# A graph layer's gathers in another order on GpSimd's queue, and its node statistics one block nearer

## The reference

```
h = maximum(layernorm(x), 0)                      # 100000 x 160
s, v = h[:, :64], h[:, 64:] as (N, 32, 3)
skip = s @ W_skip0, v @ W_skip1
s, v = s @ W_nl0, v @ W_nl1
w = relu(edge_feature @ W_fc1) @ W_fc2            # 25000 x 224, in five parts
xs, xv = s[dst], v[dst]                           # gathered by edge
tp = products of w, xs, xv and the edge's unit vector
agg = segment_sum(tp, src, N) / 32
out = agg @ W_out + skip
gate: silu on 64 scalars, sigmoid of 32 times the vectors
x + result
```

## Time and profile before

| | us |
|---|---|
| median of 3 runs | 1115.03 |
| lowest and highest run | 1113.84, 1117.93 |
| the profiled execution, device time | 1114.05 |
| its span, first to last instruction | 1112.2 |
| PE, DVE, ACT, POOL busy in the span | 1055.0, 960.1, 911.9, 762.7 |
| first and last scatter start | 147.35, 540.77 |
| first and last residual start | 555.65, 1103.40 |

### The profile page before, as it was taken

The page is one execution under the profiler, slowest core; times in us unless marked ns, Lnnn a source line. Parts: engine busy times, 40 slices in busy tenths (PEclk is TensorE's granted clock), DMA queues, the critical chain, the costliest instruction groups (busy, mean ns, idle before and its releaser), DMA issues.

```text
span 1112.2 us, 29797 instructions
## 1 busy us (share of the span) xinstructions
PE 1055.0 (95%) x8847; PEld 930.5 (84%) x8847; DVE 960.1 (86%) x3525; ACT 911.9 (82%) x2168; POOL 762.7 (69%) x1021
## 2 busy tenths in 40 slices
PE   6899899999999999789799999999999999999996
PEld 5678688888888887678698889999999899989885
DVE  9999789888888896668389899999999999999984
ACT  0796578777787876546699999999999999999994
POOL 6777777777777777775726667676767665667650
PEclk9999899999999999869699999999999999999998
DMA  9999745544455664343488788888888888888863
GB/s 336 403 403 402 255 136 137 143 135 137 139 138 143 216 230 141 109 118 103 139 295 301 281 298 308 306 310 299 312 298 313 296 297 311 302 305 308 301 215 128
DMA packets 108461, 271.14 MB, mean 244 GB/s; under 512 B 13573, under 2 KB 51751, under 8 KB 108364
## 3 DMA queue, kind: packets, MB, share of 16 engines
q1 hardware_dynamic: 87852, 233.20, 59.6%
q0 software_dynamic: 19200, 36.48, 10.8%
q10 hardware_dynamic: 1312, 0.29, 0.1%
HBM read 126.91 MB, written 143.01 MB: 243 GB/s over the span
## 4 chain that ended last, share of the span: by engine, by line
PE 36%; DVE 24%; DMA 21%; issue 7%; POOL 6%; SPq 4%; ACT 0%; DVEq 0%; POOLq 0%; ACTq 0%
DMA xb<-x 20%; DVE n_stat L995 7%; PE bank L1457 6%; DVE ob L1093 6%; DVE ob L1086 5%; PE bank L1486 4%; POOL slots L546 4%; PE bank L1388 3%; PE bank L1474 3%; PE bank L1470 3%; PE bank L1472 3%; PE bank L1494 2%; PE bank L1440 2%; DVE bin_hot L660 2%; PE bank L1527 2%
## 5 line engine op out<-in xcount | busy, mean ns | idle before, releaser
L1302 ACT ACTIVATE nn<-xb,n_bias,n_rstd 128x160 f32<-128x160 f32 x784 | 345.4, 526 | 0.0
L546 POOL DMA_INDIRECT slots<-msg,sidx x200 | 208.1, 1041 | 68.3 <-issue 57.3
L995 DVE BATCH_NORM_STATS2 n_stat<-xb 128x6 f32<-128x160 f32 x784 | 195.9, 313 | 35.6 <-DMA xb<-x 34.7
L1545 PE MATMUL bank<-mg,hot 64*128 64x192 f32 x1568 | 172.3, 338 | 2.4 <-DVE hot L1071 2.4
L530 POOL DMA_INDIRECT xg<-x,dst_i x136 | 136.3, 1002 | 43.9 <-issue 40.7
L1527 PE MATMUL bank<-fwd,nt 128*128 128x160 f32 x784 | 153.6, 319 | 8.9 <-DVE ob L1086 6.4
L595 POOL TENSOR_TENSOR n_rstd<-n_sum,neg_half 128x8 f32<-128x8 f32 x94 | 156.4, 1664 | 7.6 <-POOL n_sum L588 6.9
L1093 DVE TENSOR_TENSOR ob<-ob,xb 128x1280 f32<-128x1280 f32 x98 | 146.2, 1492 | 3.4
L1527 PEld LDWEIGHTS bank<-fwd,nt 128*128 128x128 f32 x784 | 112.5, 190 | 40.0 <-issue 33.1
L1086 DVE SCALAR_TENSOR_TENSOR ob<-sg,bank 128x128 f32<-128x128 f32 x588 | 130.9, 278 | 17.0 <-ACT ob L1320 17.0
L1312 ACT ACTIVATE nt<-bank 128x640 f32<-128x640 f32 x196 | 136.6, 698 | 9.0 <-PE bank L1536 7.3
(11 more groups left out here) (197 smaller groups left out, 2686.5 us busy)
## 6 DMA issues: line engine op xcount, KB each, us to landing
xb<-x SPq DMA_DIRECT2D x97, 640.0 KB, 5.2
out_dram<-ob SPq DMA_DIRECT2D x97, 640.0 KB, 3.3
slots<-blank SPq DMA_DIRECT2D x14, 2744.0 KB
mg<-slots SPq DMA_DIRECT2D x98, 392.0 KB, 4.0
messages<-msg SPq DMA_DIRECT2D x50, 382.8 KB
ef<-edge_feat_t SPq DMA_DIRECT2D x50, 125.0 KB
slots<-msg,sidx POOLq DMA_INDIRECT x200, 3.6
xg<-x,dst_i POOLq DMA_INDIRECT x136, 6.4
```

The costliest lines, as they stand in the source:

```text
L546: pool.indirect_dma_start(slots[:, :], bass.IndirectOffsetOnAxis(ap=sidx[:, m:m + 1], axis=0), msg[:, c, t, 0:MW], None).then_inc(e_sc[c], 16)
L995: done = dve.bn_stats(n_stat[:, u // U, u % U * G + g, :], xb[:, u, g, :])
L1302: last = act.activation(nn[:, u % 2, h, spread_of(g % 4)], xb[:, u, g, order_of(g % 4)], ACT.Relu, bias=n_bias[:, u // U, c:c + 1], scale= ...
L1545: last = pe.matmul(q_z[h][:, t, 0:Z], hot[slots, u % 2, pair, :], mg[slots, u % U, pair, 0:Z], start=False, stop=(h == 0), skip_group_chec ...
```

## The change

Three lines change, in two stages. `FIRST_GATHERS` goes from 112 to 128. Behind the scatters of each group come two gathers until all 200 are made; before, the bound `GE * (p + 11)` made it four behind groups 36 to 39. In the node stage DVE takes the statistics of block i + 5 in round i instead of i + 6, so the loop's first such round is 3 (block 8), and the last 92 (block 97).

```diff
-    FIRST_GATHERS = 112
+    FIRST_GATHERS = 128
...
-                    due = min(NT, max(FIRST_GATHERS + 2 * (p + 1), GE * (p + 11)))
+                    due = min(NT, FIRST_GATHERS + 2 * (p + 1))
...
-                        s, v = i + 6, (u + 6) % XU
-                        measure = macro_exists(s) and macro_exists(i - 2)
+                        s, v = i + 5, (u + 5) % XU
+                        measure = macro_exists(s) and macro_exists(i - 3)
```

## The result

The changed kernel takes **1087.68 us** (median of 4 runs, 1086.12 to 1088.71) where the kernel before took 1116.48 beside it (4 runs, 1113.84 to 1118.47): a ratio of 0.974, with an interval of 0.971 to 0.977. The prediction was 1092.5 in a range of 1087 to 1101. The sign and both mechanisms held, and the time lies near the range's low end: both halves gave more than they were costed at. The profiled execution of after took 1086.12 us, 27.9 less than that of before.

The account below looks back on a forecast made before the run. Bounds: node-row loads in the node stage, POOL's queue with late gathers in the edge stage. 1114.05 - 7.3 + 1.0 - 15.8 = 1091.95 us, taken as 1092.5 with the median's offset; range 1087 to 1101.

Parts of the forecast that it names:

- A: Edge stage: POOL's queue loses its waits for messages, so the node stage starts earlier: -7.3 us, bounded by 0 and -9.
- The slack of the ring: Edge stage: ACT's copy for group 44 finds its message buffer, one of eight, free with 1.5 us to spare.
- B: Node stage's start: PE's first adds stay at the lower clock for longer: +1.0 us, between 0 and +1.7.
- C: Node stage: DVE's waits for node-row loads go, rounds take 5.49 us: -15.8 us.
- the floor of 530.0: Node stage: first to last residual with rounds at PE's 5.47 us, a gain of 17.7 us.
- the slack of the even blocks' bias: Node stage: POOL has an even block's bias ready 2.9 us before ACT reads it, so ACT does not wait.
- R1: Node stage: something other than the load holds rounds, half the excess stays, rounds 5.56 us, total 1098.7 us; chance 0.09.
- R2: Edge stage: the gather change gives nothing, last scatter ends near 541 us, total 1099.3 us; chance 0.06.
- R3: Node stage: waits on node-row loads stay because loads come slower in shorter rounds, total 1107.8 us; chance 0.05.
- R4: Node stage: POOL becomes the bound and ACT waits for the bias, priced at 1145.7 us; chance 0.06.
- The three more steps held for 1.3 us each: Node stage: POOL steps held by DVE, making a pair of blocks take 12.1 us and a round 6.05; priced under R4.
- The price of a ring that runs full: Edge stage: if message buffers run out, ACT and DVE stop a few us while POOL has seven groups; cost nothing.

Follow-up runs that it names:

- e_small_store: The kernel before, statistics still six blocks ahead, storing only 1/8 of each block's output: 1095.61 us (one run).
- e_stats_only: The kernel before with only the statistics moved to block i + 5, gathers as before: 1098.87 us, ratio 0.979.
- e_gathers_only: The kernel before with only the gather change (128 first, two behind each group), statistics still six blocks ahead: 1107.66 us, ratio 0.988.
- e_late: e_stats_only with the last gathers later, four behind a group from group 40 on instead of 36: 1109.17 us (one run).
- e_warm: The changed kernel with 48 unused matmuls on PE before the node stage's first add: 1088.97 us, ratio 0.972.
- e_136: The changed kernel with 136 gathers first instead of 128: 1088.48 us, ratio 0.970.
- e_load_first: The kernel before with SyncE issuing each round's load of node rows ahead of the output store and message load: 1119.9 us, ratio 0.998.
- e_after_load_first: The changed kernel with SyncE issuing each round's load of node rows ahead of its other two transfers: 1087.13 us.
- e_four: The changed kernel with the statistics of block i + 4 in round i instead of i + 5: 1190.9 us (one run).
- e_160: The changed kernel with 160 gathers first instead of 128: 1106.14 us, ratio 0.986.

## Why the prediction was right, and where its sizes were off

**What bounds the kernel.** Right in both stages: the load in the node stage (e_small_store, e_stats_only), the gathers that stood behind scatters in the edge stage (e_gathers_only, e_late).

**A, POOL's queue.** Right, with -7.95 for -7.3 at the last scatter (532.82 us, forecast 533.4); the mean of five executions on either side is -7.8. The points on the way held as well: scatter group 36 starts at 459.65 (460.0), the statistics of the last gathered group are read at 464.56 with no wait, ACT's copy for group 44 is at 470.26 (469.9), POOL never waits over 0.3 us for a message. The slack of the ring was 1.5 us in the forecast; in the trace ACT waits 0.2 us, once. DVE's timeline of after, those statistics and the last message:

```profile
464.56 0.99 DVE L672 BATCH_NORM_STATS2 e_stat<-xg 125x6 f32<-125x160 f32 x4
...
519.64 0.16 DVE L924 COPY msg<-place_of 125x4 f32<-125x4 f32 x1
```

The last group's second half is ready at 519.8 us instead of 515, and POOL takes it at 531.55: 11.8 us in hand for the 12 of the forecast. DVE is later where PE's clock was low: in after the granted clock was 0.66 from 474 to 494 us. In e_gathers_only and e_warm, which have the same edge stage and the same statistics in it, the clock was 1.00 there and the message was ready at 513.7 and 513.6.

The term that was mis-sized is the end of A: I took the landing of 4.50 us and the load of 2.98 from the earlier trace rows unchanged. The landing became 2.37, and the load 3.19. What I missed is that the second copy's store, beside which the old last scatter ran, is also moved relative to it. Measured from first add to first add (549.36 before, 539.40 after) A is -9.96, not -7.3, which is past its bound of -9.

**B, the clock.** Forecast +1.0, measured +0.3: first add to first residual takes 6.56 us for 6.29. PE's stretches of after (length, busy, clock, DMA share, GB/s), against the earlier trace rows:

```profile
512.00:543.00 31.00, 16.70 (x78) 0.50 0.46 142
543.00:553.00 10.00, 10.00 (x94) 1.00 0.47 169
```

The low stretch is longer, as forecast, and ends at 543 for good. What counts is how much of it lies behind the first add: from 539.40 to 543 now, 3.6 us, and from 550 to 553 before, where the first add was at 549.36. These are nearly the same. I had added a second low stretch to the old one, but the new one stands in the place of the old, and the rest of it lies before the add, where PE has nothing to do.

That this came out at +0.3 is partly luck. How long the low level lasts behind the first add differs between executions of the same node stage. In e_136 the clock was 0.50 for all of the 6.0 us behind it (540.35 to 546.35), and the first residual came 7.19 us after the first add. In the kernels whose first adds run at the lower level throughout (1.65 us for the eight) the interval is 6.6 to 7.2 us, with the gathers of after as with those of before; before has 6.29, with adds of 1.39. So a difference of 0.3 or of 1.0 between two single executions says little about the change.

**C, the rounds.** Forecast 5.49 us and -15.8, measured 5.47 and -18.15. PE's 5.47 us of the earlier trace rows is the pace of the rounds. The stretch of 529.60 is even 0.4 below the floor of 530.0, because its first two rounds, which have no statistics, take 5.32 us each. The term that was mis-sized is the 5.49, chosen by ACT's 5.51. I took ACT's pace between two disturbances for ACT's own. ACT waits for PE, and PE for everything, so three rounds with small disturbances in them cannot show an engine's own pace; the last rounds, where nothing was in the way, could. The other kernels with the same rounds have stretches of 529.5 to 530.4. Those with the rounds of before have 547.75, 552.0 (e_gathers_only) and 554.6 (e_load_first, loads in front), so 18 us is the low side of what the change is worth here.

**POOL.** Right: the slack of the even blocks' bias is 3.0 to 3.1 us (forecast 2.9), of the odd 5.7 to 6.1 (5.7 to 6), its wait before a pair at most 2.8 (2.8), and ACT never waits for `n_bias`.

**The sum.** 1114.05 - 9.96 + 0.27 - 18.15 = 1086.2, for 1086.12. Of the 5.8 us by which the profiled execution beat 1091.95, 2.35 are C, 2.7 are A (2.1 of them the landing) and 0.7 are B. The sum was set up against this execution, and 1086.12 lies under the low end of 1087: A passed its bound of -9, and C the floor of -17.7. Only the median, 1.6 us above the profiled execution, falls into the range, by 0.7 us; that it does is luck, and both bounds were drawn too tight.

**The rivals.** R1 (half of the excess stays) would have shown as rounds of 5.56: they are 5.47. R2 (the edge stage gives nothing) falls with the last scatter at 532.82. R3 (the waits on the loads stay) falls with the missing wait line, and with e_after_load_first, where even a load of 6.7 us isn't seen. R4 (POOL becomes the bound) did not come, and e_four shows that it was one block away. The three more steps held for 1.3 us each that R4 needed did not appear. What happened is that the held step changed: POOL's pair now starts 0.8 us before DVE's residual instead of 0.5, so that line 582 is through before it (0.206 us at the median, for 1.523 in the earlier trace rows) and line 583 is held in its place (1.513 for 0.277). From the timeline of after, where the residual runs from 808.11 us for 1.49:

```profile
807.92 0.20 POOL L582 TENSOR_TENSOR n_sum<-n_sum 128x16 f32<-128x16 f32 x1
808.19 1.47 POOL L583 TENSOR_SCALAR n_sum<-n_sum 128x16 f32<-128x16 f32 x1
```

The Trainium skill's rule (SBUF — State Buffer, section "SBUF: two separate sides"), that DVE and GpSimd lock one pair of ports between them, agrees with this trace as it did with that of before: each time it is the step that meets the residual that takes 1.5 us.

**What the forecast did not name.** The price of a ring that runs full was put at nothing. It was harmless here because ACT waited for it only 0.2 us. For a few us the sentence holds: in e_136 ACT waits 9.5 us, at most 4.1 at once, and the time is that of after. Its reason, that POOL has seven groups in hand, does not hold: in e_160, where ACT stops for 26.2 us at once, the price is 18 us.

## What to carry to other kernels

When a load is on the chain, look at when its buffer came free and when its data is read, and move the reader by one round before touching the load: here this gave 18 us, while issuing the load earlier gave nothing. With one queue for two kinds of transfers, as POOL's here, the order is free between two limits, the consumer that starves and the ring that fills, and a lead that looks large shrinks with every round in which the consumer is faster than the producer. Take an engine's floor from rounds where nothing disturbs it, not from quiet stretches between disturbances.

## What the runs showed of the hardware

- A transfer that is issued before its round's others need not land sooner. The 640 KB load took 5.2 us (median) as the third of its round and 6.7 as the first, and the store behind it 7.7 instead of 3.3. With the store cut to 80 KB, the load took 4.5.
- The same indirect scatter of the last tile landed after 2.35 to 2.64 us where the message's other copy had been ready to store for 8 us or more, after 3.35 with 5.2 us, and after 4.30 to 5.20 with 2.1 to 2.7 us; without that store in the program it was 2.82, for 4.31.
- A POOL operation of 0.21 us (line 582) or 0.28 us (line 583) on 128x16 took 1.5 us when it met DVE's residual of 1.49 us. Which of the two it was changed with POOL's start: 0.5 us before the residual in before, 0.8 in after.
- PE's clock was at the lower level again (0.51) from 537.2 us, 3.3 us after the last of 48 matmuls, most of which had run at the full one. They ended 6.7 us before the first add and brought nothing.
